# A two-pass convolution and expert kernel: the first two tiles of a pass as one stretch, the base copies moved, more half-channel stores

## The chip, the core and the metric

The kernel runs on one core of one Trainium2 chip. The metric is the device time of one execution in microseconds (us). Engines are named as the profile names them: PE (TensorE), PEld (its weight loads), DVE (VectorE), ACT (ScalarE), POOL (GpSimd), SP (SyncE, which here only issues DMAs).

## The reference, cut to what matters

Input `x` is 8 batches x 4096 positions x 512 channels in float32. Two steps follow one another.

```python
# step 1, on all of x: a long convolution per channel over the normalised input
x = x + conv(layernorm(x)) + layernorm(x) * omega      # 8 x 4096 x 512
# step 2, on 4096 tokens (1024 x 4) read from the result: two of eight experts per token
h  = gelu(xr @ w1A[e].T @ w1B[e]);  ye = h @ w2A[e].T @ w2B[e]
x  = x + y          # y: the weighted sum of the two experts, scattered to the tokens
```

(The experts' tokens are the first 4096 rows of the flattened array, which are all of batch 0. In the kernel `T` is 4096, and `o_tok` is the output seen as rows of 512 channels.)

## The kernel before, in words

**Passes, tiles, blocks, units.** The convolution is done in two passes `g` = 0 and 1, four batches each. A pass has four tiles `t` of 128 channels (DG = 4). A tile has 8 blocks `i` (BT = 8), a block has two units `k` of 8 channels, so 16 units a tile (UT = 16). `xb` has two halves; a tile lives in one half (128 partitions x 128 rows x 128 channels, 8 MB), is computed in place, and is stored from there, while the other half takes the next tile.

**One unit.** POOL and DVE each centre half of a unit's channels (L581, L1225, `cen`), DVE multiplies by the reciprocal deviation (L1236, `xn`), PE forms chunk sums (L1448) and local products (L1461), ACT shifts (L947) and builds tap matrices (L966, L967, L973), DVE scans the state (L1263), PE adds the part between chunks (L1473), and DVE adds the result into `xb` (L1247, the function `add`, which raises `s_ev` by one). In the loop the add of unit u-1 stands behind the scan of unit u. At the end of each tile DVE's function `steps` (with `end`) does the last add first and only then centres and stages the first unit of the next tile (L1272 on); PE's `over_halves` likewise closes the last unit of each tile before it starts the next. This is done for every tile of a pass, by `over_tile_blocks` and `over_halves`.

**SP's queue.** All tile loads and stores and the weights of the blocks are issued by SP in program order (`tile(g, t, first, final)`). A tile is moved in 16 pieces. In the first tile of a pass SP loads the next tile (16 pieces of 512 KB, L679) and then, once 8 units are added, stores the first 64 of the tile's 128 channels (16 half pieces of 256 KB, L786; runs of 64 channels are 256 bytes). In the second tile it waits for the 16th add of the first tile, stores the other halves (16 x 256 KB), and loads the third tile into the half that they leave. In the third tile it stores the second tile in whole pieces (16 x 512 KB, runs of 512 bytes, L696) and loads the fourth tile; each load waits for the store of its own piece (`s_put`). In the fourth tile it stores the third. Between the pieces stands a pair of weight loads per block (L736, 256 KB and L738, 128 KB).

**End of pass 0 and the experts.** In the fourth tile of pass 0 SP loads `w2a` (L769), stores four first halves into `y_d` (the rows the experts read, YP = 4 pieces) and issues three of the four base copies `copy_out` (L791: 1024 rows x 384 channels from `y_d` to `out`, 1.5 MB each); then `w1a` (L805), the slot table (L808) and, after the last add, the four second halves into `y_d` (L786). When they are there, POOL gathers the rows of the first two of 39 expert tiles (L613). An expert tile on PE is `turn`, `rank`, `up`, `down`, `widen`. DVE takes statistics of the gathered rows (`token_stats`, L1293), normalises them (L1302) and copies the rank result (`rank_in_half`, L1307, L1309), without which the next expert tile's `up` (L1556) cannot start. POOL's `tile(q)` scatters the result of tile q-3 to `out` (L548; at q = 3 only after all four base copies and four whole stores `store_last` have landed), then computes the deviation of tile q+2 (L621, L623) and gathers tile q+3 (L613), in this order. SP's `up_load(q)` waits until `up` of tile q-2 is done.

**End.** In the last tile of pass 1 SP stores the first 64 channels (16 half pieces) after 8 adds and the other 64 after the last add (the loop at L860).

## Time and profile before

| | us |
|---|---|
| median of 3 runs | 1139.38 |
| the three runs | 1147.12, 1139.38, 1137.70 |
| the profiled execution's own time | 1141.59 |
| span in its trace | 1139.8 |

The profiled execution has 1.8 us outside the span and is 2.2 us above the median. Busy shares over the span: PE 81%, DVE 72%, ACT 69%, POOL 53%; the mean granted TensorE clock is 0.941 of full speed. Pass 0 runs from about 121 to 388 us, the experts from there to about 850, pass 1 from there to the end. In the profile's 40 slices each slice is 28.5 us, a digit is a tenth of the slice.

### The profile page before, as it was taken

Reading aid. Unit: us, or ns where it says so; the run is one execution under the profiler, and the core shown is the slowest. Engines: PE = TensorE matmul, PEld = TensorE weight load, DVE = VectorE, ACT = ScalarE, POOL = GpSimd, SP = SyncE. Lnnn points to the kernel's source line nnn. Section 1 sums busy time; section 2 is a strip of 40 time slices with the busy share of each in tenths; the row PEclk is TensorE's granted clock in tenths of the full one; section 3 lists DMA queues with packets and bytes.
Section 4 is the critical chain, followed back from the end, with each engine's and each line's share of the span. In section 5 each row is a group of like instructions: output and inputs, shape, how many; then the busy total and the mean of one; then the engine's idle time right before and its main releaser. Section 6 shows DMA issues by size and latency. Waiting matters only on the chain. (4 is left out here: it accounts for less than half of the span.)

```text
span 1139.8 us, 32813 instructions
## 1 busy us (share of the span) xinstructions
PE 921.1 (81%) x11452; PEld 745.4 (65%) x11452; DVE 815.8 (72%) x1360; ACT 784.9 (69%) x1151; POOL 602.2 (53%) x674
## 2 busy tenths in 40 slices
PE   2770588879858858999999999999987888885882
PEld 1540477767747746777777777777766777774671
DVE  6877897988859533565767767776657989795891
ACT  2782698979949734656565566565667989896890
POOL 4334785868755133656666666665665433331330
PEclk9995798999979979999999999999999999898896
DMA  7999799999999986999999999899749999999986
GB/s 254 387 401 334 198 264 220 259 251 287 265 287 322 266 211 182 240 262 290 275 267 245 230 249 245 225 251 233 177 107 263 221 207 265 268 291 255 312 191 150
DMA packets 391625, 288.01 MB, mean 253 GB/s; under 512 B 125416, under 2 KB 339080, under 8 KB 391042
## 3 DMA queue, kind: packets, MB, share of 16 engines
q1 hardware_dynamic: 347458, 211.88, 69.9%
q0 software_dynamic: 19520, 36.26, 14.6%
q10 hardware_dynamic: 24576, 38.94, 10.5%
q8 instruction: 43, 0.70, 0.3%
q14 instruction: 28, 0.23, 0.1%
HBM read 197.41 MB, written 100.61 MB: 261 GB/s over the span
## 5 line engine op out<-in xcount | busy, mean ns | idle before, releaser
L1461 PE MATMUL ps<-xn,wb 128*128 128x128 f32 x2048 | 275.4, 290 | 0.0
L1062 ACT ACTIVATE cen<-ps 128x1024 f32<-128x1024 f32 x156 | 155.8, 1024 | 169.1 <-PE ps L1556 169.0
L581 POOL TENSOR_TENSOR cen<-xb,mean 128x512 f32<-128x512 f32 x128 | 143.0, 1118 | 228.5 <-DVE state L1263 160.9
L1461 PEld LDWEIGHTS ps<-xn,wb 128*128 128x128 f32 x2048 | 250.6, 200 | 17.4 <-issue 3.1
L1236 DVE TENSOR_TENSOR xn<-cen,rstd 128x1024 f32<-128x1024 f32 x128 | 174.5, 1363 | 51.0 <-POOL cen L581 39.4
L1448 PE MATMUL ps<-xn,near 128*32 128x128 f32 x2048 | 86.8, 289 | 134.4 <-DVE xn L1236 84.9
L1556 PE MATMUL ps<-carry,wb 64*128 64x256 f32 x1248 | 168.7, 400 | 13.0 <-DVE carry L1309 10.9
L1571 PE MATMUL ps<-cen,xn 128*64 128x128 f32 x2496 | 160.4, 276 | 0.4 <-ACT cen L1062 0.3
L1571 PEld LDWEIGHTS ps<-cen,xn 128*64 128x64 f32 x2496 | 135.9, 137 | 37.7 <-ACT cen L1062 30.7
L1247 DVE TENSOR_TENSOR xb<-xb,ps 128x1024 f32 (+1 forms) x128 | 152.9, 1194 | 9.9 <-PE ps L1473 9.9
L966 ACT ACTIVATE wb<-wide 32x1024 f32<-32x1024 f32 x126 | 144.4, 1146 | 16.6 <-DMA wide<-taps_d 14.0
L1448 PEld LDWEIGHTS ps<-xn,near 128*32 128x32 f32 x2048 | 52.4, 113 | 157.3 <-issue 73.8
L1556 PEld LDWEIGHTS ps<-carry,wb 64*128 64x128 f32 x1248 | 112.5, 188 | 42.5 <-issue 25.6
L1293 DVE BATCH_NORM_STATS2 tstat<-wide 128x6 f32<-128x512 f32 x78 | 53.9, 694 | 118.4 <-DMA wide<-y_d,pick_g 118.4
L967 ACT ACTIVATE wb<-wide 32x768 f32<-32x768 f32 x126 | 114.8, 911 | 1.5
L613 POOL DMA_INDIRECT wide<-y_d,pick_g x78 | 89.1, 1142 | 46.5 <-POOL pick_g L610 34.6
L465 POOL DMA_INDIRECT slot_d<-rowf,posi x64 | 103.2, 1613 | 10.4 <-issue 10.3
L1225 DVE TENSOR_TENSOR cen<-xb,mean 128x512 f32<-128x512 f32 x128 | 91.4, 714 | 17.1 <-DMA xb<-L_attn_x 17.1
L1473 PE MATMUL ps<-state,carry 32*128 32x128 f32 x2048 | 93.5, 297 | 0.0
L1094 DVE BATCH_NORM_STATS2 wb<-xb 128x512 f32 (+1 forms) x128 | 78.5, 679 | 18.8 <-DMA xb<-L_attn_x 18.4
L947 ACT ACTIVATE shift_s<-ps,coef 128x124 f32<-128x124 f32 x128 | 45.5, 356 | 64.5 <-PE ps L1448 63.4
L1473 PEld LDWEIGHTS ps<-state,carry 32*128 32x128 f32 x2048 | 69.0, 186 | 25.1 <-issue 24.1
(173 smaller groups left out, 1262.0 us busy)
## 6 DMA issues: line engine op xcount, KB each, us to landing
xb<-L_attn_x SPq DMA_DIRECT2D x96, 512.0 KB
out<-xb SPq DMA_DIRECT2D x72, 512.0 KB, 6.5
xb<-L_attn_x SPq DMA_DIRECT2D x32, 1024.0 KB, 10.0
xb<-L_attn_x ACTq DMA_DIRECT2D x128, 256.0 KB, 4.9
out<-xb SPq DMA_DIRECT2D x88, 256.0 KB, 4.5
wb<-L_ffn_w_B SPq DMA_DIRECT2D x78, 256.0 KB, 4.5
wide<-taps_d SPq DMA_DIRECT2D x62, 256.0 KB, 6.1
dk<-decay_d SPq DMA_DIRECT2D x62, 128.0 KB, 5.4
```

The lines of the kernel that those rows point to most:

```text
L465: pool.indirect_dma_start(out=slot_d, out_offset=bass.IndirectOffsetOnAxis(ap=pos_col[:, c:c + 1], axis=0), in_=row_col[:, 2 * c:2 * c + 2 ...
L581: pool.tensor_tensor(cen[:, k, 0:QB // 2].rearrange("p b r d -> p r b d"), unit_view(pool, g, i, k)[:, :, 0:UC // 2] .rearrange("p r (b d) ...
L966: act.activation(dst[0:ZR], src, ACT.Copy)
L967: act.activation(dst[ZR:2 * ZR, :, :, ZR:P], src[:, :, :, 0:P - ZR], ACT.Copy).then_inc(s_rev, 1)
L1062: act.activation(act_h[:, b % 2].rearrange("p f t -> p (f t)"), ps[:, 2 * (b % 2):2 * (b % 2) + 2, :].rearrange("p a t -> p (a t)"), ACT.G ...
L1236: dve.tensor_tensor(xn[:, k].rearrange("p (b d) r -> p b d r", d=2), cen[:, k].rearrange("p b r d -> p b d r"), rstd[:, g * P:(g + 1) * P] ...
L1247: dve.tensor_tensor(view, view, ps[:, QB * k:QB * k + QB, 0:2 * P] .rearrange("p b (d r) -> p r b d", d=2), ALU.add).then_inc(s_ev, 1)
L1448: ins = pe.matmul(ps[b * 2 * N:(b + 1) * 2 * N, QB * k, 2 * P:3 * P], near[:, h, k * QB + b, d:d + 2, :].rearrange("p z n -> p (z n)"), xn ...
L1461: ins = pe.matmul(ps[:, QB * k + b, d * P:(d + 1) * P], wb[:, h, k * QB + b, d, :], xn[:, k, 2 * b + d, :], start=(b > 0 and d == 0), stop ...
L1473: ins = pe.matmul(ps[:, QB * k + b, d * P:(d + 1) * P], carry[rows, k, d * P:(d + 1) * P], state[rows, k, :], start=False, stop=True, skip ...
L1556: ins = pe.matmul(ps[:, 2 * (b % 2) + h, f * QT:(f + 1) * QT].rearrange("p (a t) -> p a t", a=2), w1bs[half_rows, k, c * P:(c + 1) * P], r ...
L1571: ins = pe.matmul(ps[h * RANK:(h + 1) * RANK, 4, 0:P], w2as[:, (f // 2) * (FC // 2) + 2 * b + f % 2, :], act_h[:, b % 2, f, side * P:(side ...
```

## The change

Three things are changed.

1. `RUNS = ((0, 2), (2, 3), (3, 4))`: DVE and PE run through the first two tiles of each pass as one loop; the stretch's closing steps stand after tile 2, 3 and 4 of a pass, not after the first.
2. In the last block of the second tile SP issues the first halves of 8 of its 16 pieces (`SOON` = 8); in the third tile the other halves of these 8 pieces follow in place of whole pieces. In the last tile of pass 1 the early part of a piece is 80 channels (`LASTC`), issued after 10 adds, and the late part 48.
3. The three base copies leave the fourth tile of pass 0; all four now stand between the `up_load`s of the first expert tiles, and the four `store_last` stand in pairs behind the second and third of them.

```diff
+    SOON = PIECES // 2
+    LASTC = 5 * P // 8
...
+        RUNS = ((0, 2), (2, 3), (3, 4))
+
         def over_tile_blocks(eng, g, step):
 
-            for t in range(g * DG, (g + 1) * DG):
-                step(t * BT, True, False)
-                with eng.Fori(t * BT + 1, (t + 1) * BT - 1) as i:
+            for a, z in RUNS:
+                i0, i1 = g * NK + a * BT, g * NK + z * BT
+                step(i0, True, False)
+                with eng.Fori(i0 + 1, i1 - 1) as i:
                     step(i, False, False)
-                step((t + 1) * BT - 1, False, True)
+                step(i1 - 1, False, True)
+
+        def halves_out(g, tile):
+
+            return 16 * (g * (PIECES + SOON + YP) + PIECES + (0, SOON, SOON, SOON + (YP, PIECES)[g])[tile])
...
-            pool.wait_ge(s_early, 16 * (PIECES + YP))
+            pool.wait_ge(s_early, halves_out(0, DG - 1))
...
-                second = t == g * DG + 1
+                second, third = t == g * DG + 1, t == g * DG + 2
...
-                        elif second and 0 <= j < PIECES:
+                        elif (second and 0 <= j < PIECES) or (third and 0 <= j < SOON):
                             store_part(g, t - 1, j, slice(P // 2, P), s_put[j])
                         elif not first and 0 <= j < PIECES:
                             store_tile(g, t - 1, [j])
                         elif PIECES <= j < 2 * PIECES and not first and not final:
-                            if second and j == PIECES:
-                                sp.wait_ge(s_early, 16 * (PIECES if g == 0 else 2 * PIECES + YP))
+                            if j == PIECES:
+                                sp.wait_ge(s_early, halves_out(g, t - 1 - g * DG))
                             load_tile(g, t + 1, [j - PIECES], stored(g, t - 1))
-                    if final and g == 0 and b >= BT // 2:
-                        if b == BT // 2:
-                            for j in range(PIECES):
-                                sp.wait_ge(s_put[j], 16 * t)
-                            for j in range(KC):
-                                sp.dma_start(load2a[:, j, :], w2a[j * P:(j + 1) * P, :]).then_inc(s_wl, 16)
-                            store_early(g, t, range(YP))
-                        else:
-                            copy_out(b - BT // 2)
+                    if second and b == BT - 1:
+                        for j in range(SOON):
+                            store_part(g, t, j, slice(0, P // 2), s_early)
+                    if final and g == 0 and b == BT // 2:
+                        for j in range(PIECES):
+                            sp.wait_ge(s_put[j], 16 * t)
+                        for j in range(KC):
+                            sp.dma_start(load2a[:, j, :], w2a[j * P:(j + 1) * P, :]).then_inc(s_wl, 16)
+                        store_early(g, t, range(YP), P // 2)
                     if final and g == 1 and b == BT - 1:
-                        store_early(g, t, range(PIECES))
-
-            def store_early(g, t, pieces):
-
-                sp.wait_ge(s_ev, UT * t + UT // 2)
+                        store_early(g, t, range(PIECES), LASTC)
+
+            def store_early(g, t, pieces, cols):
+
+                sp.wait_ge(s_ev, UT * t + cols // UC)
                 for j in pieces:
-                    store_part(g, t, j, slice(0, P // 2), s_early)
+                    store_part(g, t, j, slice(0, cols), s_early)
...
             sp.wait_ge(s_w2b, 32)
-            for j in range(YP):
-                store_last(j)
             copy_out(0)
             for q in range(2, 5):
                 up_load(q, q % 2)
+                copy_out(q - 1)
+                for j in range((q - 2) * YP // 2, min((q - 1) * YP // 2, YP)):
+                    store_last(j)
...
-                store_part(1, NT - 1, j, slice(P // 2, P), s_put[j])
-            sp.wait_ge(s_early, 16 * (YP + 3 * PIECES))
+                store_part(1, NT - 1, j, slice(LASTC, P), s_put[j])
+            sp.wait_ge(s_early, halves_out(1, DG - 1))
```

(PE's `over_halves` takes the same `RUNS`.)

SP's order around the turn from the second to the third tile of pass 0. `xb<-L_attn_x` is a piece of a tile load, `y_d<-xb` and `out<-xb` are stores, `x64` at the end of a shape is a half piece and `x128` a whole one, `wide` and `dk` are a block's weights. Before:

```order
L736 DMA wide<-taps_d 32x8x256
L738 DMA dk<-decay_d 128x256
L736 DMA wide<-taps_d 32x8x256
L738 DMA dk<-decay_d 128x256
L696 DMA y_d<-xb 128x8x128 x4
L736 DMA wide<-taps_d 32x8x256
L738 DMA dk<-decay_d 128x256
L696 DMA out<-xb 128x8x128 x5
```

Now:

```order
L745 DMA wide<-taps_d 32x8x256
L747 DMA dk<-decay_d 128x256
L795 DMA y_d<-xb 128x8x64 x4
L795 DMA out<-xb 128x8x64 x4
L745 DMA wide<-taps_d 32x8x256
L747 DMA dk<-decay_d 128x256
L795 DMA y_d<-xb 128x8x64 x4
L745 DMA wide<-taps_d 32x8x256
L747 DMA dk<-decay_d 128x256
L795 DMA out<-xb 128x8x64 x4
L705 DMA out<-xb 128x8x128
```

Eight half pieces stand ahead of the last weights of the second tile, and eight more take the place of eight whole ones behind them.

DVE's order at a turn between tiles (L1247 is `add`, L1263 the scan, L1225 `centre`, L1236 `stage`). Before, this stands behind every tile of a pass but the last:

```order
L1263 SCALAR_TENSOR_TENSOR state<-carry,shift_s 128x128
L1247 TENSOR_TENSOR xb<-xb,ps 128x128x8 x2
L1225 TENSOR_TENSOR cen<-xb,mean 128x128x2x2
L1236 TENSOR_TENSOR xn<-cen,rstd 128x1024
L1225 TENSOR_TENSOR cen<-xb,mean 128x128x2x2
L1236 TENSOR_TENSOR xn<-cen,rstd 128x1024
```

Now, between the first and the second tile, the loop's body runs on:

```order
L1246 TENSOR_TENSOR xn<-cen,rstd 128x1024
L1235 ISA
L1235 TENSOR_TENSOR cen<-xb,mean 128x128x2x2
L32 REGISTER_ALU
L1273 SCALAR_TENSOR_TENSOR state<-carry,shift_s 128x128
L32 REGISTER_ALU
L1257 ISA x2
L1257 TENSOR_TENSOR xb<-xb,ps 128x128x8
```

The 16th add of the first tile, which stood right behind the 15th, now stands behind the scan of the second tile's first unit.

SP's order at the start of the experts, from the `w2b` load (L833) on; `wb<-L_ffn_w_B` is a half of an `up_load`. Before (after the second `up_load`, with its four stores and one copy in one piece):

```order
L818 DMA wb<-L_ffn_w_B 64x1024
L823 DMA out<-xb 128x8x128 x4
L791 DMA out<-y_d 1024x384
L373 TENSOR_LOAD t_e
L373 ISA x2
L818 ISA
L818 DMA wb<-L_ffn_w_B 64x1024
```

Now, from the same `up_load` to the third copy:

```order
L800 DMA out<-y_d 1024x384
L375 TENSOR_LOAD t_e
L375 ISA x2
L827 ISA
L827 DMA wb<-L_ffn_w_B 64x1024
L827 ISA
L827 DMA wb<-L_ffn_w_B 64x1024
L800 DMA out<-y_d 1024x384
L832 DMA out<-xb 128x8x128 x2
L375 TENSOR_LOAD t_e
```

The fourth copy now stands behind `up_load(4)`, so behind SP's wait for the `up` of the third expert tile.

## Rows read from the trace of the kernel before

**Rows 1.** The page, part 2: DMA, 40 slices of 28.5 us, tenths.

```profile
DMA  7999799999999986999999999899749999999986
```

**Rows 2.** Timeline, DVE, first turn of pass 0 (start, us, instruction, idle before).

```profile
178.61 0.86 DVE L1263 TENSOR_TENSOR_SCAN state<-carry,shift_s 128x128 f32<-128x128 f32 x1
...
184.81 1.22 DVE L1247 TENSOR_TENSOR xb<-xb,ps 128x1024 f32<-128x1024 f32 x1 [1.22 <-PE ps L1473]
...
198.77 0.42 DVE L1263 TENSOR_TENSOR_SCAN state<-carry,shift_s 128x128 f32<-128x128 f32 x1
...
202.63 0.41 DVE L1263 TENSOR_TENSOR_SCAN state<-carry,shift_s 128x128 f32<-128x128 f32 x1
```

**Rows 3.** Timeline, DVE, first turn of pass 1.

```profile
911.94 0.41 DVE L1263 TENSOR_TENSOR_SCAN state<-carry,shift_s 128x128 f32<-128x128 f32 x1
...
917.69 1.22 DVE L1247 TENSOR_TENSOR xb<-xb,ps 128x1024 f32<-128x1024 f32 x1 [1.10 <-PE ps L1473]
...
927.13 0.41 DVE L1263 TENSOR_TENSOR_SCAN state<-carry,shift_s 128x128 f32<-128x128 f32 x1
...
934.51 0.41 DVE L1263 TENSOR_TENSOR_SCAN state<-carry,shift_s 128x128 f32<-128x128 f32 x1
```

**Rows 4.** Timeline, POOL and DVE, the second turns of both passes.

```profile
247.84 1.10 POOL L581 TENSOR_TENSOR cen<-xb,mean 128x512 f32<-128x512 f32 x1 [4.66 <-DMA xb<-L_attn_x]
...
248.81 1.22 DVE L1247 TENSOR_TENSOR xb<-xb,ps 128x1024 f32<-128x1024 f32 x1 [1.28 <-PE ps L1473]
...
979.21 2.16 POOL L581 TENSOR_TENSOR cen<-xb,mean 128x512 f32<-128x512 f32 x2 [5.49 <-DMA xb<-L_attn_x]
...
980.48 1.22 DVE L1247 TENSOR_TENSOR xb<-xb,ps 128x1024 f32<-128x1024 f32 x1 [1.09 <-PE ps L1473]
```

**Rows 5.** Timeline, DVE, the third turns of both passes.

```profile
322.90 0.69 DVE L1225 TENSOR_TENSOR cen<-xb,mean 128x512 f32<-128x512 f32 x1 [8.15 <-DMA xb<-L_attn_x]
...
1053.93 0.69 DVE L1225 TENSOR_TENSOR cen<-xb,mean 128x512 f32<-128x512 f32 x1 [8.96 <-DMA xb<-L_attn_x]
```

**Rows 6.** Windows: stretch, engines' busy time, PEclk, DMA share, GB/s (last two).

```profile
187.00:248.00 61.00, 54.32 (x756) 46.20 (x756) 52.91 (x62) 56.25 (x79) 44.12 (x37) 0.94 1.11 257
248.00:251.00 3.00, 0.66 (x17) 0.47 (x16) 2.19 (x2) 1.17 (x2) 2.81 (x3) 1.00 0.20 47
251.00:323.00 72.00, 54.88 (x768) 46.68 (x768) 55.33 (x65) 57.14 (x80) 45.57 (x39) 0.91 1.11 275
979.00:983.00 4.00, 1.33 (x23) 1.02 (x21) 2.82 (x4) 2.01 (x3) 2.16 (x2) 0.90 0.71 155
1056.00:1082.00 26.00, 21.98 (x307) 18.64 (x308) 23.21 (x27) 22.49 (x32) 8.90 (x10) 0.91 1.09 315
1121.00:1138.00 17.00, 0.00 (x0) 0.00 (x0) 0.00 (x0) 0.00 (x0) 0.00 (x0) 0.53 0.97 216
```

**Rows 7.** Timeline, SP, the second halves into `y_d`, behind the three base copies.

```profile
387.80 7.86 SPq L786 DMA_DIRECT2D y_d<-xb  x4
```

**Rows 8.** Timeline, POOL, the first gather and the first scatter.

```profile
398.60 0.19 POOL L610 COPY pick_g<-slot_g 128x2 int32<-128x2 int32 x1 [19.33 <-DMA y_d<-xb]
...
454.77 0.20 POOL L541 COPY pick_s<-slot_s 128x2 int32<-128x2 int32 x1
```

**Rows 9.** Timeline, PE and DVE, the third expert tile and `rank_in_half(5)`.

```profile
442.17 3.08 PE L1556 MATMUL ps<-carry,wb 64*128 64x256 f32 x16 [4.46 <-DVE carry L1309]
...
450.78 1.13 PE L1556 MATMUL ps<-carry,wb 64*128 64x256 f32 x8
...
474.50 0.29 DVE L1307 COPY carry<-ps 128x128 f32<-128x128 f32 x1 [1.04 <-PE ps L1541]
```

**Rows 10.** Source L791 (the four base copies), issue to landing.

```profile
DMA to landing us min/median/max: 10.3/13.6/19.3
```

**Rows 11.** Timeline, DVE, the last tile: its 10th and 16th add.

```profile
1097.41 1.19 DVE L1247 TENSOR_TENSOR xb<-xb,ps 128x1024 f32 x1
...
1117.30 1.22 DVE L1247 TENSOR_TENSOR xb<-xb,ps 128x1024 f32<-128x1024 f32 x1 [1.42 <-PE ps L1473]
```

More of the change, by code:

```diff
@@ L76, in build @@
     YP = CH // PR
-    assert YP % 2 == 0
+    assert YP % 2 == 0 and DG == 4
+    SOON = PIECES // 2
+    LASTC = 5 * P // 8
     ZR = P // 4
@@ L567, in tile_start @@
             def tile_start(i, g):
-                return isinstance(i, int) and i % BT == 0 and i != g * NK
+                return i - g * NK in [a * BT for a, _ in RUNS[1:]]
             def centres(g):
@@ L1487, in over_halves @@
             def over_halves(g):
-                for t in range(g * DG, (g + 1) * DG):
-                    steps(t * BT, 0, True)
-                    with pe.Fori(t * BT // 2, (t + 1) * BT // 2 - 1) as p:
+                for a, z in RUNS:
+                    i0, i1 = g * NK + a * BT, g * NK + z * BT
+                    steps(i0, 0, True)
+                    with pe.Fori(i0 // 2, i1 // 2 - 1) as p:
                         steps(p * 2 + 1, 1)
                         steps(p * 2 + 2, 0)
-                    steps((t + 1) * BT - 1, 1)
-                    between((t + 1) * BT - 1, 1)
+                    steps(i1 - 1, 1)
+                    between(i1 - 1, 1)
             pe.wait_ge(s_late, NLATE)
```

## The prediction

> **What bounds the kernel now.** I read the slices first [rows 1]. DMA stands at 9 tenths or more in nearly every slice of both passes, which makes its queue the first suspect, but a share says nothing of who waits. Then the turns between tiles.
>
> *First turn* [rows 2, 3]. DVE scans once a unit: 198.77 and 202.63 are one unit apart, 3.86 us; 927.13 and 934.51 two units, 3.69 us each. From the scan at 178.61 to the one at 202.63 are five units: 24.0 us instead of 19.3, so the turn costs 4.7 us. In pass 1, 911.94 to 934.51 is 22.6 instead of 18.4: 4.1 us. This is what the run-through can take away, 8.8 us together.
>
> *Second turn* [rows 4]. POOL centres the first unit of the third tile as soon as its load has landed: it waited for the DMA until 247.84, and the last add of the second tile ended at 250.03. In pass 1: 979.21 and 981.70. The loads are there only 2.2 and 2.5 us before the compute wants them.
>
> *Third turn* [rows 5]. Here the compute waits in earnest: DVE has idled 8.15 us, its adds all done, when the fourth tile's load lands at 322.9, and 8.96 us in pass 1 at 1053.9. So each pass is set by the DMA at its third turn, and whatever is won before it is lost in this wait unless the loads land earlier too.
>
> *What sets these loads* [rows 6]. The window 187 to 248, in which SP stores halves and loads the third tile, has a DMA share of 1.11 throughout, and so has 251 to 323. Between them, 248 to 251, it is 0.20: SP waits for the last add. The queue is a chain of work: last add of tile 1, second halves, load of tile 3, a short hole, stores of tile 2, load of tile 4.
>
> **The change, part by part.**
>
> *1. The run-through, first effect: the last add is later.* In the loop the add of unit 15 stands behind the scan of unit 16. Pass 0: 178.61 is the scan of unit 14, two units later is 186.3, the add starts 0.3 behind it, 186.6 instead of 184.81 [rows 2]: 1.8 us later. Pass 1: 911.94 + 7.4 + 0.3 = 919.6 instead of 917.69 [rows 3]: 2.0 us later. SP waits for this add before its second halves, and behind them stand the loads of the third tile, on a full queue. So these land at 247.84 + 1.8 = 249.6, and at 981.2. The second tile's compute ends 4.7 us earlier (4.1), at about 245.3 and 977.6, and now waits for the loads: of the 8.8 us nothing is left but some 1 us at the start of the third tile, which the third turn's wait absorbs.
>
> *2. The hole closes.* The second tile's last add (245.3) is now earlier than the end of the loads, and SP has issued eight half stores as well. It is worth, by the windows, 3 x (1 - 0.20/1.11) = 2.5 us in pass 0 and 4 x (1 - 0.71/1.11) = 1.4 us in pass 1 [rows 6]. The run-through alone would have closed it.
>
> *3. Eight pieces in halves.* A half store costs 16 x 256 KB at 216 GB/s, 1.21 us each, with only such stores running (1121 to 1138) [rows 6]. For a whole one I compare the two chains of a pass, which differ only in 16 whole for 16 half stores: last add to landed load, 186.03 to 247.84 is 61.8 us and 250.03 to 322.9 is 72.9, in pass 1 60.3 (918.91 to 979.21) and 72.2 [rows 2 to 5] (an add lasts 1.22); so a whole one costs 0.69 to 0.74 us more than a half, about 1.93. Two halves are 2.42, 0.5 us more. Eight pieces: 4.0 us a pass. Ends: a whole piece at the 315 GB/s of the window 1056 to 1082 is 1.66 us, so 0.76 x 8 = 6.1 us; and 0, if in the mixed stream bytes alone count, as nearly in the first window (257 GB/s with 16 half stores in it, against 275). I take 4.0, from the stretch in which these stores will stand.
>
> What the rows give for two halves against a whole is 2.42 against 1.93 at the least. The Trainium skill (DMA: Bandwidth & Descriptors, Why small descriptors are slow) counts a fixed 3 cycles per descriptor beside one per 32 bytes, so 22 for two halves against 19; by it, an estimate, term 3 would be 2.4 us a pass (1.93 x 3/19 x 8) and the whole sum 3.2 us less. The trace asks for more, and the measurement decides.
>
> Third turn: pass 0 1.8 - 2.5 + 4.0 = **+3.3 us**, pass 1 2.0 - 1.4 + 4.0 = **+4.6 us**. Where the compute idled 8 to 9 us at this turn it will idle 15 to 17: the TensorE clock, 0.91 over these windows, will fall for longer, which costs nothing that isn't in the turn already.
>
> *4. Base copies out of the fourth tile.* They are ahead of the four `y_d` halves, whose issue took 7.86 us on the full queue [rows 7] and whose landing released the first gather at 398.60 [rows 8], 10.8 us after the last add. On an empty queue four halves need 0.9 + 4 x 1.21 + 1.0 = 6.7 us (start and tail as at the kernel's end: last add 1118.5, 16 x 1.21, end 1139.8 [rows 11]): 394.5. The slot table and PE's transposes, which the gather needs too, may then be the later ones; I allow 0.6 us: 395.1. Gain **-3.5 us**; ends -2 (the `w1a` load still ahead) and -4.5.
>
> *5. The copies in the expert loop.* SP issues, behind `w2b`, copy, `up_load(2)`, copy, two stores: 0.5 MB more ahead of the gather for tile 3 than four stores and one copy, on a queue which already holds PE up by 4.46 us before 442.17 [rows 9]. At 250 to 290 GB/s that is 1.8 us; between 0 and 3 I take **+1.0**. The rest of the copies go against a wait: POOL's first scatter (454.77 [rows 8], now 452.3 by the two terms) waits for all four. The fourth is behind `up_load(4)`, which waits for the `up` that ended at 451.9 [rows 9], now 449.4; issued at 451.5. The four copies took 10.3 to 19.3 us to land, 13.6 in the middle [rows 10]; the quickest had 1 MB of halves (4.8 us) ahead, the new one 0.5 MB of `up_load` (1.9 us), so 7.4 at least; I take 9: 460.5. POOL stands still 8 us, and behind it in its queue are the deviation of tile 5 and the gather of tile 6. DVE takes that gather's statistics before `rank_in_half(5)`, which PE needs for the next expert tile. The slack there is 1.04 us of DVE idle at 474.50 [rows 9]; I allow 2.2 us for a quicker landing on an emptier queue and for PE's own lag behind DVE's copies: 460.5 - 452.3 = 8.2, less 1.0 and 2.2, gives some **+4.5 us**, once, since POOL keeps pace afterwards. Ends 0 (it lands with the 452.3) and +9.
>
> *6. The last stores.* The early part may start after the 10th add, 1098.6 [rows 11], two units later than before, and then fills the queue until the last add: 1098.6 + 0.9 + 16 x (80-channel + 48-channel run) + 1.0. On a line through 1.21 us for 256 bytes and 1.66 to 1.93 for 512 the two are together 2.42: 38.7 us, end 1139.2 against 1139.8: **-0.6 us**. Ends: -1.5, if the early run is done when the last add ends, and +3 (rival D).
>
> Instruction counts otherwise fall by a few waits; the half stores' extra SP issues stand beside a full queue and cost nothing of their own.
>
> Sum: 3.3 + 4.6 - 3.5 + 1.0 + 4.5 - 0.6 = **+9.3 us**. Against the median of 1139.4 that is **1148.7 us**; the profiled execution before, 1141.6, lies 2.2 above its median and would become 1150.9.
>
> **The rivals.**
>
> *A. The halves cost nothing and the copies are hidden (0.2).* Terms 3 and 5 at their lower ends: -0.7 + 0.6 - 3.5 - 0.6 = -4.2, 1135.2; with the scatter wait alone 1140. For it: the mixed windows move nearly the same GB/s.
>
> *B. Faster: the compute, not the queue, sets the third turn (0.1).* If the loads move up with the compute, because SP's order is paced by the block's weights and not by a full queue, both turns come off: -8.8 - 3.5 - 0.6 = -12.9, 1126.5. It decides if the third tile's loads would land more than 4 us earlier than the compute asked for them; the rows say 2.2 and 2.5 and a share of 1.11.
>
> *C. Slower (0.12).* A half store is worth its 1.21 and a whole one 1.66, +12.2 for both passes, and the scatter waits 9 us: +18, 1157. It decides if the fourth copy lands later than about 462.
>
> *D. The last runs don't divide (0.08).* If a 48-channel run costs what a 64-channel run does (1.21 us a piece) and an 80-channel one 1.4, a fifth of the way from 1.21 to 1.93 and more, the end is 16 x 2.61 = 41.8 us after the start, 3.1 later than with 38.7: 1151.8. No row has such a run. The Trainium skill (DMA: Bandwidth & Descriptors, How a descriptor splits into AXI transactions) speaks for this case: a read starts at a 256-byte boundary and is billed for the bytes ahead of its own start, and the late run begins at byte 320 of a 512-byte row.
>
> *E.* That the run-through does nothing, because the second tile's loads aren't there, is out: SP issues them in the first four blocks of the first tile, half a tile ahead of the turn.
>
> **The numbers.** The forecast itself has 0.5, from 1143 to 1155. The range that should hold 8 in 10 is 1136 to 1158: from A's end to C. 1% of 1139.4 is 11.4 us, about what can be told from no change. Faster than 1128: B, 0.10. Slower than 1150.8: two fifths of the forecast's half (0.2), C and half of D, 0.36. Within 1%: the rest, 0.54.
>
> **What would show it.** The wait of DVE for the load at the third turns grows from 8 and 9 us to about 15, with the loads landing 3 to 5 us later after the pass's start; the DMA hole at the second turn is gone. The last add before the second halves comes 2 us later. The first gather starts 7.3 us after the last add of pass 0 instead of 10.8. POOL's first scatter waits some 8 us for the DMA, and PE stalls by 4 to 5 us before its sixth expert tile. Wrong would be: loads that land earlier at the third turn (then B), a scatter that doesn't wait, or an end more than 21 us behind the last add.

## The result, and the profile after

The changed kernel took **1156.77 us** (median of 4 runs, 1156.35 to 1157.85), the one before 1141.73 (4 runs, 1137.7 to 1147.12): a ratio of 1.013, with an interval of 1.0083 to 1.0178. So it is slower, by 15 us, where 1148.7 was forecast and the range ended at 1158. The profiled execution took 1157.0 with a span of 1155.2; the span before was 1139.8. The 15.4 us between the two spans are what is explained here.

The page first, part 2: busy tenths in 40 slices, the granted clock and the DMA.

```profile
span 1155.2 us, 33019 instructions
...
PEclk9995799989969979899999999999999999897896
DMA  7999899999999489889999999899749989999969
```

The DMA row is as full as it was [rows 1]. It can't show what changed; one line of part 3 can. Of the kernel's 408258 packets 158440 are below 512 bytes, and before there were 125416: 33024 more, and 32768 of them are the half pieces (16 whole pieces of 1024 runs each have become two halves of 1024 runs).

The second turn of pass 0: DVE's last add of the second tile, then the load it waits for (start, us, instruction, and in brackets the idle time before it with what ended it).

```profile
245.19 1.22 DVE L1257 TENSOR_TENSOR xb<-xb,ps 128x1024 f32<-128x1024 f32 x1 [1.30 <-PE ps L1483]
250.90 0.69 DVE L1235 TENSOR_TENSOR cen<-xb,mean 128x512 f32<-128x512 f32 x1 [4.49 <-DMA xb<-L_attn_x]
250.95 1.59 POOL L590 TENSOR_TENSOR cen<-xb,mean 128x512 f32<-128x512 f32 x1 [11.39 <-DMA xb<-L_attn_x]
```

The run-through did what it says. The tile's last add starts at 245.19 instead of 248.81 [rows 4] (245.3 was forecast), and DVE then stands still for 4.49 us, because the load lands at 250.9 instead of 247.8. The gain of the first turn is handed over to the queue within one tile.

The third turns, pass 0 and pass 1, from the last add on.

```profile
314.50 1.22 DVE L1257 TENSOR_TENSOR xb<-xb,ps 128x1024 f32<-128x1024 f32 x1 [0.93 <-PE ps L1483]
330.04 0.69 DVE L1235 TENSOR_TENSOR cen<-xb,mean 128x512 f32<-128x512 f32 x1 [14.31 <-DMA xb<-L_attn_x]
...
1054.04 1.22 DVE L1257 TENSOR_TENSOR xb<-xb,ps 128x1024 f32<-128x1024 f32 x1 [1.09 <-PE ps L1483]
1067.23 0.69 DVE L1235 TENSOR_TENSOR cen<-xb,mean 128x512 f32<-128x512 f32 x1 [11.97 <-DMA xb<-L_attn_x]
```

These answer to [rows 5]: 8.15 us of waiting have become 14.31, and 8.96 have become 11.97. Windows of the same stretches (busy time of PE, PEld, DVE, ACT and POOL, then granted clock, DMA share, GB/s):

```profile
190.00:251.00 61.00, 49.30 (x724) 41.97 (x720) 50.38 (x59) 54.14 (x76) 44.21 (x35) 0.97 1.14 257
251.00:330.00 79.00, 53.85 (x768) 45.83 (x768) 55.83 (x64) 57.56 (x80) 50.69 (x40) 0.89 1.07 252
```

Against [rows 6] the same 768 matmuls now stand in 79 us instead of 72, the DMA share is 1.07 for 1.11, and the queue moves 252 GB/s where it moved 275. Nothing of the hole of 3 us is left (248 to 251 us has a share of 1.17, where it had 0.20), and still the load lands later.

The start of the expert loop: SP's halves into `y_d` behind the last add, and POOL's first gather.

```profile
394.85 2.92 SPq L795 DMA_DIRECT2D y_d<-xb  x4
402.40 0.18 POOL L619 COPY pick_g<-slot_g 128x2 int32<-128x2 int32 x1 [16.09 <-DMA y_d<-xb]
```

The issue of the four second halves takes 2.92 us instead of 7.86 [rows 7], and the gather starts 7.6 us behind the last add (394.82) instead of 10.8 [rows 8]. Then the fourth base copy on SP, POOL's first scatter, which waits for it, and DVE and PE at the sixth expert tile.

```profile
456.51 0.59 SPq L800 DMA_DIRECT2D out<-y_d  x1
...
465.06 0.18 POOL L550 COPY pick_s<-slot_s 128x2 int32<-128x2 int32 x1 [3.32 <-DMA out<-y_d]
...
481.10 0.69 DVE L1303 BATCH_NORM_STATS2 tstat<-wide 128x6 f32<-128x512 f32 x1 [1.83 <-DMA wide<-y_d,pick_g]
...
485.10 1.23 PE L1567 MATMUL ps<-carry,wb 64*128 64x256 f32 x4 [5.41 <-DVE carry L1319]
```

The scatter had no wait before [rows 8]. PE's third expert tile (its `up`, at 443.86) is 41.5 us behind the first gather instead of 43.6, the fourth (458.11) 55.7 instead of 56.0, and the sixth 82.7 instead of 77.5: all of the loss stands at the sixth. The copies now took 8.4 to 14.0 us to land, 10.1 in the middle; before 10.3 to 19.3 [rows 10].

Last, the stores at the end: the last add, and two windows, one with the 80-channel parts and one with the 48-channel parts.

```profile
1131.08 1.22 DVE L1257 TENSOR_TENSOR xb<-xb,ps 128x1024 f32<-128x1024 f32 x1 [1.42 <-PE ps L1483]
```

```profile
1120.00:1132.00 12.00, 10.36 (x160) 8.81 (x159) 8.75 (x10) 6.27 (x11) 1.60 (x2) 1.00 1.29 240
...
1134.00:1154.00 20.00, 0.00 (x0) 0.00 (x0) 0.00 (x0) 0.00 (x0) 0.00 (x0) 0.51 0.96 166
```

A 48-channel part holds 192 KB, so at 166 GB/s it takes 1.18 us, hardly less than the 1.21 us of a 64-channel part with its 256 KB [rows 6]. An 80-channel part takes 320 KB / 240 GB/s = 1.37 us. (Here 1 KB is 1024 bytes and 1 GB is 10^9.) The end comes 22.9 us behind the last add, 21.3 before.

Where the 15.4 us are, read from the same marks in both traces:

| stretch | before | after | change | sum |
|---|---|---|---|---|
| up to the first add of pass 0 | 131.84 | 133.10 | +1.3 | 1.3 |
| to the landed load of the fourth tile | 322.95 | 330.09 | +5.9 | 7.1 |
| to the first gather | 398.60 | 402.40 | -3.3 | 3.8 |
| to the sixth expert tile on PE | 476.13 | 485.10 | +5.2 | 9.0 |
| to the first add of pass 1 | 859.39 | 869.96 | +1.6 | 10.6 |
| to the landed load of the fourth tile | 1053.97 | 1067.28 | +2.7 | 13.3 |
| to the last add's end | 1118.52 | 1132.30 | +0.5 | 13.8 |
| to the end of the span | 1139.8 | 1155.2 | +1.6 | 15.4 |

The first row lies ahead of anything that was changed, so a row of such a table is uncertain by 1 us at the least. In the expert loop it is more: a second profile of the same kernel (the last experiment) has the sixth expert tile 87.2 us behind the gather where this one has 82.7.

The lower granted clock (0.930 over the span, 0.941 before) isn't a cause. From its landed load to its last add the fourth tile of pass 0 took 64.8 us before and 64.7 after, and in pass 1 64.6 and 65.0.

### The profile page after: what moved, and what is told of

It reads as the page before. It is cut to its first block and busy times, and to the rows that moved or that the text cites. A ratio compares the mean times of both kernels' runs of the same rounds, so it can differ in the third digit from the quotient of the medians.

```text
span 1155.2 us, 33019 instructions
## 1 busy us (share of the span) xinstructions
PE 921.4 (80%) x11452; PEld 744.5 (64%) x11452; DVE 817.4 (71%) x1360; ACT 784.8 (68%) x1151; POOL 609.2 (53%) x674
## 2 busy tenths in 40 slices
DMA packets 408258, 287.91 MB, mean 249 GB/s; under 512 B 158440, under 2 KB 355720, under 8 KB 407682
## 3 DMA queue, kind: packets, MB, share of 16 engines
q1 hardware_dynamic: 364098, 211.88, 70.8%
q10 hardware_dynamic: 24576, 38.94, 10.3%
## 5 line engine op out<-in xcount | busy, mean ns | idle before, releaser
L1246 DVE TENSOR_TENSOR xn<-cen,rstd 128x1024 f32<-128x1024 f32 x128 | 177.1, 1384 | 45.6 <-POOL cen L590 38.6
L474 POOL DMA_INDIRECT slot_d<-rowf,posi x64 | 109.6, 1713 | 10.6 <-issue 10.6
```

Of the source, the lines that this page charges most:

```text
L474: pool.indirect_dma_start(out=slot_d, out_offset=bass.IndirectOffsetOnAxis(ap=pos_col[:, c:c + 1], axis=0), in_=row_col[:, 2 * c:2 * c + 2 ...
L1246: dve.tensor_tensor(xn[:, k].rearrange("p (b d) r -> p b d r", d=2), cen[:, k].rearrange("p b r d -> p b d r"), rstd[:, g * P:(g + 1) * P] ...
```

## The experiments

Three sets of four kernels. The kernel before, run beside each set, took 1139.27, 1154.44 and 1162.03 us, so times are compared only as ratios to it; 0.01 is 11.4 us in the first set and 11.6 in the third. Most of the difference between the sets lies in the expert loop: from the sixth expert tile to the first add of pass 1 the kernel before needs 383.3 us, the one divided by rows, in the third set, 400.1. Why, no run shows; that the first and the third set bear the same chip number speaks against the chip. A diff is against the changed kernel unless it says otherwise. "Copies as before" is

```diff
-                    if final and g == 0 and b == BT // 2:
+                    if final and g == 0 and b >= BT // 2:
...
+                        else:
+                            copy_out(b - BT // 2)
...
+            for j in range(YP):
+                store_last(j)
             copy_out(0)
             for q in range(2, 5):
                 up_load(q, q % 2)
-                copy_out(q - 1)
-                for j in range((q - 2) * YP // 2, min((q - 1) * YP // 2, YP)):
-                    store_last(j)
```

### Set 1: the parts, one by one

**The run-through alone** (copies as before, and)

```diff
-    SOON = PIECES // 2
-    LASTC = 5 * P // 8
+    SOON = 0
+    LASTC = P // 2
```

> The kernel before with the run-through of the first two tiles of each pass alone: whole pieces, last stores 64/64 and base copies as before. Queue theory (the DMA queue sets the third turn): the 8.8 us of compute come off but are lost in the wait for the fourth tile's loads; third turn -0.7 us in pass 0 and +0.6 in pass 1, so the time is that of before within 2 us, and DVE's idle before the fourth tile grows from 8 and 9 us to 12 or 13. Rival (the compute sets it): 8 to 9 us faster than before.

Measured 1138.08 us, 0.998 (0.9957 to 1.0002). POOL at the second and the third turn of pass 0:

```profile
249.61 1.59 POOL L590 TENSOR_TENSOR cen<-xb,mean 128x512 f32<-128x512 f32 x1 [11.51 <-DMA xb<-L_attn_x]
...
320.37 1.59 POOL L590 TENSOR_TENSOR cen<-xb,mean 128x512 f32<-128x512 f32 x1 [12.63 <-DMA xb<-L_attn_x]
```

The first load lands 1.8 us later than in [rows 4], just what the later add costs, and the second one 2.6 us earlier than in [rows 5]. Of the 8.8 us of the two first turns nothing reaches the time that can be told from none. The idle time was expected wrongly, though. DVE waits 4.61 us at the second turn, where it had no wait, and 5.72 and 6.72 us at the third turns, not 12 or 13: it is done with the third tile at 314.6 us where the kernel before was at 314.7, because what the first turn gave was already handed back at the second.

**No early halves** (everything else as changed)

```diff
-    SOON = PIECES // 2
+    SOON = 0
```

> The changed kernel with its extra half stores undone (no first halves in the second tile's last block, whole pieces in the third tile). If two halves cost 0.5 us more than a whole piece: 8 us faster than the changed kernel, about 1.1490 ms where that is at 1.1568; from the third turns measured after the change (5.8 and 3.1 us late instead of the 3.3 and 4.6 forecast) 8 to 10 us. If the halves cost nothing and it is their order or the later last add that holds the loads: the time of the changed kernel within 2 us.

Measured 1143.15 us, 1.0031 (1.001 to 1.0052). Against 1.013 of the changed kernel some 0.01 is gone, 11 us, with nothing but the eight half pieces of each pass. The fourth tile's load in pass 0:

```profile
323.62 1.59 POOL L590 TENSOR_TENSOR cen<-xb,mean 128x512 f32<-128x512 f32 x1 [13.58 <-DMA xb<-L_attn_x]
...
458.75 0.18 POOL L550 COPY pick_s<-slot_s 128x2 int32<-128x2 int32 x1 [5.71 <-DMA out<-y_d]
```

The load lands 6.5 us earlier than the changed kernel's. The wait of the scatter stays, so it belongs to the copies.

**The last tile at 64 and 64**

```diff
-    LASTC = 5 * P // 8
+    LASTC = P // 2
```

> The changed kernel with its last stores of pass 1 split 64/64 channels again, the early part after 8 adds. In the trace after, an 80-channel part takes 1.37 us a piece (240 GB/s) and a 48-channel one 1.18 (166 GB/s), together 2.55 against 2.42, and the end came 22.9 us behind the last add instead of 21.3: 1.6 us faster than the changed kernel. If the split is worth what the forecast said, 0.6 us slower.

Measured 1154.87 us, 1.0156 (1.0134 to 1.0177), not to be told from the changed kernel's 1.013. The trace does tell: the last add ends at 1130.45 and the span at 1151.8, 21.4 us later, where the changed kernel has 22.9. The 80/48 division costs 1.5 us in its own place.

**The copies back**

> The changed kernel with the base copies where they were before (three in the fourth tile of pass 0, one behind the four whole stores). By the traces the move gained 3.3 us up to the first gather (7.6 us behind the last add instead of 10.9) and lost 5.2 up to the sixth expert tile, so undoing it gives 2 us, and no wait of the first scatter for a DMA. Rival: the 1.6 us that the later expert tiles lost too belong to it, then 3.5 us; or the loss has other grounds, then it gets 3 us slower.

Measured 1151.66 us, 1.0117 (1.0099 to 1.0135). The gather starts 10.1 us behind the last add, as before the change. POOL's first scatter:

```profile
456.33 0.19 POOL L550 COPY pick_s<-slot_s 128x2 int32<-128x2 int32 x1
```

No wait. The sixth expert tile is 77.9 us behind the first gather instead of 82.7. So by these traces the move wins 2.5 to 3.3 us at the gather and loses 4.8 to 5.2 behind it. The two times (1.0117 and 1.013) can't be told apart.

### Set 2: what a half piece costs, and the last runs

**Only the division.** The kernel before, but eight whole pieces of the third tile's stores are issued in place as two channel halves:

```diff
+                            if third:
+                                store_part(g, t - 1, j, slice(0, P // 2), s_early)
                             store_part(g, t - 1, j, slice(P // 2, P), s_put[j])
```

> The kernel before (no run-through, copies and last stores as before); in each pass's third tile 8 of the 16 pieces are stored as two halves, one right behind the other, at the place of the whole piece. It asks what the shorter runs cost by themselves. By the size alone, 0.5 us a piece as forecast: 8 us slower than before, the third turns 4.0 us later each. From the pair of kernels with and without early halves (third tile's load to fourth tile's load 79.1 against 71.7 us and 76.6 against 72.2): 7.4 and 4.5 us, 12 us slower. If the cost came from their place, right behind the loads, and not from their size: as before within 2 us.

Measured 1168.73 us, 1.013 (1.0091 to 1.0169): 15 us. The window of the stores, first of the kernel before and then of this one:

```profile
250.00:281.00 31.00, 25.76 (x352) 21.93 (x352) 27.04 (x32) 25.13 (x36) 22.40 (x21) 0.89 1.00 272
```

```profile
249.00:285.00 36.00, 31.55 (x416) 26.70 (x416) 32.58 (x38) 31.06 (x43) 31.02 (x24) 0.91 1.01 244
```

The same 16 pieces take 36 us instead of 31, with the engines as busy (1.01, 1.00) and fewer GB/s. That is 5 us, 0.63 a piece, in pass 0. By the landed loads it is 4.0 us in pass 0 (326.95 for 322.95) and 5.6 in pass 1 (80.4 us from the third tile's load to the fourth's, for 74.8). The time says 7.5 a pass; what the rest is isn't shown.

At the start of these stores the pieces into `y_d` are at the head of SP's queue, whole in the kernel before (first window) and halves here:

```profile
251.00:256.00 5.00, 2.83 (x24) 2.42 (x25) 4.79 (x6) 1.56 (x3) 1.51 (x2) 0.58 1.01 281
```

```profile
251.00:256.00 5.00, 5.00 (x44) 4.34 (x40) 3.50 (x5) 3.65 (x5) 3.28 (x4) 0.50 0.94 207
```

At 281 GB/s a whole piece takes 1.87 us, at 207 GB/s a half takes 1.27, so two halves are 0.67 us dearer.

**The early halves without the run-through** (copies as before, 64 and 64, and)

```diff
-        RUNS = ((0, 2), (2, 3), (3, 4))
+        RUNS = ((0, 1), (1, 2), (2, 3), (3, 4))
```

> The kernel before with the early halves alone (first halves of 8 pieces in the second tile's last block, second halves in the third tile; no run-through, copies and last stores as before). Size theory: the time of the kernel with the split alone, less the part of the hole at the second turn that the early halves fill (2.5 and 1.4 us by the windows, 4.3 and 3.0 by the run-through's own trace): between 3 and 8 us slower than before. Place theory: slower than the split alone. Were the halves free, as their place in the diff suggests, it would be 4 to 7 us faster than before.

Measured 1162.54 us, 1.0059 (1.0035 to 1.0083): 7 us. Where the first halves can fill the hole they cost less than in place, but they cost. (The two intervals don't overlap. In the traces the difference is in pass 1, 77.6 us from load to load for 80.4; in pass 0 the loads land at 326.55 and 326.95.) DVE and POOL stand still for 12.53 and 19.65 us at the third turn of pass 0, whose load lands at 326.55.

**The last tile in three parts** (the kernel before, with 64, 32 and 32 channels)

```diff
-    LASTC = 5 * P // 8
+    LASTC = 3 * P // 4
...
-                        store_early(g, t, range(PIECES), LASTC)
+                        store_early(g, t, range(PIECES), P // 2)
+                        sp.wait_ge(s_ev, UT * t + LASTC // UC)
+                        for j in range(PIECES):
+                            store_part(g, t, j, slice(P // 2, LASTC), s_early)
```

> The kernel before with the last tile of pass 1 stored in three parts: 64 channels after 8 adds, 32 after 12, the last 32 after the last add (runs of 256, 128 and 128 bytes; the middle one begins at byte 256 of a 512-byte row, the last at byte 384). It prices short runs. If a run costs by what it moves: each 32-channel part 0.6 to 0.8 us a piece, 10 to 13 us for 16, and the end 6 us earlier behind the last add than 21.3. If a short run costs what 256 bytes cost: 1.2 us both, 19 us each, and the end no earlier; as the middle part (issued at 1112, done at 1131) is then still running at the last add (1118.5), 10 us later. If reads start at 256-byte boundaries and nothing else counts: the middle part 0.8 us a piece, the last one 1.2.

Measured 1156.08 us, 1.0007 (0.9981 to 1.0033). Two windows, the first within the second parts (channels 64 to 95, which start at byte 256 of a row), the others within the last (96 to 127, byte 384):

```profile
1137.00:1139.00 2.00, 0.00 (x0) 0.00 (x0) 0.00 (x0) 0.00 (x0) 0.00 (x0) 0.84 1.12 169
...
1145.00:1147.00 2.00, 0.00 (x0) 0.00 (x0) 0.00 (x0) 0.00 (x0) 0.00 (x0) 0.50 1.13 171
```

Both move 170 GB/s, 0.77 us a part of 128 KB. A run of 128 bytes costs the same at either place. The Trainium skill (DMA: Bandwidth & Descriptors, How a descriptor splits into AXI transactions) would bill the part at byte 384 also for the 128 bytes ahead of it; this case doesn't show that. The last 16 parts need 12.3 us, but the 16 before them start only at about 1130, when the 64-channel parts are through, and so both stand behind one another in the last 25 us; the end is 19.7 us behind the last add (1135.8).

**One copy in the fourth tile, the last one behind the second `up_load`** (run-through, whole pieces, 64 and 64)

```diff
+                    if final and g == 0 and b == BT // 2 + 1:
+                        copy_out(1)
...
-            for q in range(2, 5):
+            for q in range(2, 4):
                 up_load(q, q % 2)
-                copy_out(q - 1)
-                for j in range((q - 2) * YP // 2, min((q - 1) * YP // 2, YP)):
+                copy_out(q)
+                for j in range((q - 2) * YP // 2, (q - 1) * YP // 2):
                     store_last(j)
+            up_load(4, 0)
```

> A version that may beat both: the run-through, whole pieces, last stores 64/64, one base copy left in the fourth tile of pass 0 and three in the expert loop, the last of them behind up_load(3) instead of up_load(4). Expected: the run-through alone (2 us faster than before), and 3 us more from the first gather (8 us behind the last add of pass 0 instead of 11), with no wait of the first scatter for a copy: 5 us faster than before. If the queue at the expert loop's start is the bound wherever the copies stand: as the run-through alone.

Measured 1153.0 us, 0.9966 (0.9939 to 0.9992). The gather and the scatter:

```profile
396.23 0.18 POOL L619 COPY pick_g<-slot_g 128x2 int32<-128x2 int32 x1 [16.25 <-DMA y_d<-xb]
...
455.16 0.19 POOL L550 COPY pick_s<-slot_s 128x2 int32<-128x2 int32 x1
```

The gather is 7.7 us behind the last add (388.49) and the scatter doesn't wait: both sides at once. No copy stands behind `up_load(4)` any longer, which waits for PE; but one copy fewer stands there, too, and no run has the one without the other. By the time this kernel can't be told from the run-through alone (0.998).

### Set 3: the copies alone, and what of a half piece costs

**The copies moved, nothing else** (as the run without early halves, and `RUNS` and `LASTC` as before)

> The kernel before with the base copies moved alone (all four and the paired whole stores between the up_loads; no run-through, whole pieces, last stores 64/64). Forecast's steps: 3.5 us won up to the first gather, 5.5 lost up to the sixth expert tile by the wait of the first scatter: 2 us slower than before. From the earlier pair with and without the move (the two kernels with run-through and whole pieces, less 1.6 us of last stores): 3.5 us slower. If the wait is harmless: 3 us faster.

Measured 1166.22 us, 1.0038 (1.0007 to 1.0069), 0.8 to 8 us.

```profile
394.37 0.19 POOL L619 COPY pick_g<-slot_g 128x2 int32<-128x2 int32 x1 [15.77 <-DMA y_d<-xb]
...
459.80 0.18 POOL L550 COPY pick_s<-slot_s 128x2 int32<-128x2 int32 x1 [8.06 <-DMA out<-y_d]
```

The scatter waits 8.06 us. So this part of the change is enough for the wait, and with the copies back there was none.

**The same eight pieces divided by rows**, not by channels: as many DMAs as in the run with the channel halves, but runs of 512 bytes.

```diff
-                            store_part(g, t - 1, j, slice(0, P // 2), s_early)
-                            store_part(g, t - 1, j, slice(P // 2, P), s_put[j])
+                            store_rows(g, t - 1, j, 0, s_early)
+                            store_rows(g, t - 1, j, 1, s_put[j])
```

> As the split-alone kernel, but each of the 8 pieces of a third tile is cut into two DMAs by rows (4 rows each, all 128 channels, runs of 512 bytes) instead of by channels. It tells the length of the runs from the number of DMAs: both kernels issue the same number of DMAs with the same bytes. If run length is what costs: as before within 2 us, where the split by channels was 1.3% slower. If each DMA on the full queue has a cost of its own: about as slow as the split by channels, 12 to 15 us.

Measured 1160.76 us, 0.9995 (0.9972 to 1.0019), and in the window of the stores:

```profile
249.00:285.00 36.00, 29.54 (x410) 25.32 (x411) 32.09 (x39) 30.27 (x43) 28.55 (x23) 0.95 0.99 272
```

272 GB/s, as undivided (the kernel before has 271 in the same window). Eight more DMAs a pass cost nothing that can be told; 256-byte runs in place of 512-byte ones are what costs 15 us.

**The best version** (the one-copy kernel, and of eight pieces 32 channels more after the 12th add)

```diff
                         store_early(g, t, range(PIECES), LASTC)
+                        sp.wait_ge(s_ev, UT * t + 3 * P // 4 // UC)
+                        for j in range(PIECES // 2):
+                            store_part(g, t, j, slice(LASTC, 3 * P // 4), s_early)
...
-                store_part(1, NT - 1, j, slice(LASTC, P), s_put[j])
+                store_part(1, NT - 1, j, slice(3 * P // 4 if j < PIECES // 2 else LASTC, P), s_put[j])
```

> The best of what the runs point to: run-through, whole pieces, one base copy left in the fourth tile of pass 0 (0.3% faster than before in the last call), and the last tile stored as 64 channels of all pieces after 8 adds, 32 channels of 8 pieces after 12 adds, the rest after the last add. A 32-channel part took 0.76 us a piece, so the 8 middle parts (6.1 us) fit between the end of the early ones and the last add, and behind it stand 8 x 0.76 + 8 x 1.21 = 15.8 us instead of 19.4: the end 17.7 us behind the last add instead of 21.3, 3.6 us more, 7 to 8 us faster than before in all. If the middle parts are still on the queue at the last add, the gain is less than 2 us.

Measured 1153.43 us, 0.9937 (0.9911 to 0.9963), 7 us faster than the kernel before. Against the one-copy kernel (0.9966) the times don't tell a gain, the trace does. The window behind the last add (which ends at 1133.51; the span ends at 1150.5):

```profile
1134.00:1149.00 15.00, 0.00 (x0) 0.00 (x0) 0.00 (x0) 0.00 (x0) 0.00 (x0) 0.52 1.13 201
```

The end is 17.0 us behind the last add, 21.3 before: 8 x 0.77 + 8 x 1.21 = 15.8 us of stores instead of 19.4.

**The changed kernel again**

> The changed kernel once more, on the chip on which the base copies alone are timed, since the chips differ by over a per cent in the time of the kernel before: 1.3% slower than before (interval of the first measurement 0.8 to 1.8%), 13 to 17 us; of these the copies alone 2 to 4.

Measured 1181.79 us, 1.0164 (1.0128 to 1.0199), with the third turn's load at 328.64 and a scatter that waits 6.87 us. The sixth expert tile is 87.2 us behind the gather.

## Why the prediction came out as it did

The time was in the range, near its upper edge, and the main mechanism was the forecast one: the queue sets the third turns, the halves cost it more than the hole gives, and the scatter waits for the moved copies. The greatest chance, 0.54, stood on a difference within 1%; what came, 1.3%, lay in the 0.36. The spans differ by 15.4 us where the sum was 9.3. By the table the 6.1 us between them are: the third turn of pass 0 +2.6 (5.9 for 3.3), the end +2.2 (1.6 for -0.6), the start and the rest of the expert loop, for which there was no term, +1.3 and +1.6, pass 1 up to its last add -1.4 (3.2 for 4.6), and the copies -0.2 (1.8 for 2.0).

**The run-through and the hole (1.8 - 2.5 and 2.0 - 1.4): right, nearly nothing is left.** Of the eight kernels whose runs stay at 512 bytes, the fourth tile's load of pass 0 lands at 320.4 to 323.8 in all, and the means are 322.8 with the run-through (four kernels) and 322.9 without it (the kernel before and three more). The forecast was -0.7. The load of the third tile came 1.8 us later, as forecast, once the 1.3 us at the start are taken off. From one load to the next the queue needs less without the hole than its share in a window told: with the run-through alone 70.8 and 71.8 us instead of 75.1 and 74.8, so 4.3 and 3.0 us, not 2.5 and 1.4. Not all of that is the hole: from 249 to 285 us, where the whole pieces are stored, the queue moves 284 to 298 GB/s in the five kernels without a hole and 271 to 280 in the three with one. Why isn't shown. One kernel without the run-through (the three parts), whose third load landed late, at 251.71, has 71.7 us as well; its hole was gone by itself. That fits a queue that sets both loads, and a hole that only takes up slack.

**The idle time at the third turns: one step counted twice.** The forecast had DVE wait 15 to 17 us there, the old 8 to 9 with the 4 to 5 us of the first turn and the later load on top. But its own step before had given the first turn's gain back at the second turn. So it came: DVE waits 4.49 and 4.66 us at the second turns, is done with the third tile at 315.7 us instead of 314.7, and the wait at the third turn grows only by what the load is late. It is 14.31 us in pass 0 because the load came 7.1 us later there, and 11.97 in pass 1. That the first is near the forecast's 15 is luck. The sum of the forecast didn't use this step.

**The halves (4.0 a pass): too little.** With early halves and the run-through (four profiles, two of them of the changed kernel) the fourth tile's load of pass 0 lands at 330.1, 328.5, 326.4 and 328.6, in the mean 328.4 and 5.6 us later than with whole pieces; measured from the third tile's load it is 78.1 us for 71.3, so 6.7. In pass 1 the way from the third tile's load to the fourth's is 76.6, 75.8, 75.2 and 76.0 with halves and 71.8, 72.2, 70.5 and 69.8 without: 4.8 us. That is 10.4 to 11.5 us for 8.0, or 0.6 to 0.8 us a piece; halves in place, without the run-through, cost 4.0 and 5.6. The forecast had 0.5 between bounds of 0 and 0.76. The times say 11 us by 1.013 against 1.0031, and 15 both by the halves in place and by the second measurement of the changed kernel (1.0164). So the term was right in kind and too small, and the measured price isn't firmer than these figures.

The price of a whole piece isn't one number, and that is the step that was too simple. By the two windows from 251 to 256 us, both behind a hole, a whole piece costs 1.87 us and not 1.93, and a half 1.27 and not 1.21: 0.67 a piece, 5.3 us a pass. Without the hole the whole pieces move faster, 284 to 298 GB/s from 249 to 285 us, but the kernels with early halves and the run-through have 234 to 241 there, no more than the 244 of the halves in place. So the halves also take away what the closed hole would have given, which fits their 6.7 us from load to load against 4.0 in place. The 1.93 came from two chains, 72.9 less 61.8 us [rows 2 to 5]. Both start on a queue that is idle for a microsecond, so that time falls out of the difference:

```profile
186.00:187.00 1.00, 0.00 (x0) 0.00 (x0) 0.91 (x3) 0.00 (x0) 0.00 (x0) 0.96 0.19 34
250.00:251.00 1.00, 0.00 (x0) 0.00 (x0) 1.00 (x2) 0.00 (x0) 0.97 (x2) 1.00 0.05 7
```

The rule of the Trainium skill that was weighed here (DMA: Bandwidth & Descriptors, Why small descriptors are slow), by which it would be 2.4 us a pass, an estimate, is further off than the rows were. It counts runs, not DMAs, and in that the run divided by rows agrees (0.9995).

**The copies (-3.5, +1.0, +4.5, together +2.0): the sum was right in the first trace, partly by luck.** The gather came 7.6 us behind the last add (7.3 forecast), and so it did in every kernel with the copies moved (7.3 to 7.6). The +1.0 for a later third expert tile didn't come: that tile was 2.1 us earlier behind the gather, and the fourth 0.3. All the loss stood at the sixth tile, where PE stood still for 5.41 us: 5.2 us later behind the gather, where the two terms had 5.5. And the scatter waited 3.32 us, where 8 was forecast. It started no later than forecast (62.7 us behind the gather; the forecast's 460.5 less 395.1 is 65.4), but POOL itself came to it 3.2 us later than before (59.3 us behind the gather for 56.2), since the statistics that its work ahead of the scatter needs came 3.0 us later; 3.2 and 3.32 together are the delay of the scatter. In the other kernels with the copies moved the scatter waits 3.8 to 8.1 us, and the sixth tile is 79.9 to 87.2 us behind the gather, where the kernels with the copies in their old place have 77.0 to 79.6.

The move costs more behind the sixth tile, for which no step was in the sum. In the first set the way from the first gather to the first add of pass 1 is 467.6, 465.1 and 464.4 us with the copies moved and 460.8, 459.2 and 459.0 without. That is 6.0 us in the mean, less 3.2 won at the gather, so 2.8. In the third set it is 483.9 (the copies alone) and 495.6 (the changed kernel again) against 477.0 (divided by rows), so the cost varies much from one profile to the next. By the time the copies alone cost 4.4 us, with an interval of 0.8 to 8, and the pair of run-through alone (0.998) and no early halves (1.0031) gives 5.8 less the 1.5 of the last stores, so 4.3.

**The last stores (-0.6): wrong, in sign.** An end more than 21 us behind the last add was a sign of being wrong, and it is 22.9. Rival D happened, by two thirds: the end came 1.6 us later by the table and 1.5 by the experiment, where D had +2.5. A line through 256 and 512 bytes was no way to price 192 and 320: they cost 1.18 and 1.37 us, together 2.55, where the line gave 2.42, and 16 of each make 2.1 us. The rule of the Trainium skill that was named beside D (DMA: Bandwidth & Descriptors, How a descriptor splits into AXI transactions), a run that is billed from the boundary ahead of it, agrees with the 192-byte run but not with the 32-channel parts, so it isn't shown.

**Rivals.** A (halves free, copies hidden) fell with the run without halves and with the scatter's wait. B (compute sets the third turn) fell with the run-through alone: the fourth tile's loads didn't follow the 4 to 5 us of the first turn (2.6 us earlier in pass 0 in that kernel, none in the mean of four), and the time shows no gain that can be told. C was the nearest in its total, 1157. Its price for a half piece, 0.76, and the forecast's 0.5 lie on either side of most of the measured ones (0.5 to 0.8 by the loads), and its scatter wait of 9 us is met by no run. The total was reached by D's stores and by 2.9 us that no case had, so it is luck that the time met C's.

## What to carry to other kernels

When a queue sets the time of a turn, a gain of the engines ahead of it is given back at the next load, and an edit that costs the queue more than the hole that it fills is a loss; so price the queue's items first, in the mix and at the fill of the queue in which they will stand. Divide a transfer along the dimension that keeps its runs long, and where it must be along the short one, measure each length: here 32 channels were worth dividing off and 48 were not. A transfer that another engine waits for should not stand behind an instruction on the same queue that itself waits for a late engine.

## What the runs showed of the hardware

- Stores from SBUF to DRAM with nothing else on the queues, by the length of a run: 128 bytes 170 GB/s, 192 bytes 166, 256 bytes 216. The 80-channel parts (320 bytes), which ran beside the last units' compute, moved at 240 GB/s. A 192-byte piece takes 1.18 us and a 256-byte piece 1.21, so a quarter fewer bytes gain next to nothing; a 128-byte piece takes 0.77.
- The DMA share says nothing of this: it is 1.00 at 272 GB/s with whole pieces and 1.01 at 244 GB/s with halves.
- In the same 5 us of two kernels, behind a stretch with an idle queue, stores in runs of 512 bytes moved at 281 GB/s and in runs of 256 bytes at 207. Where no such stretch lay ahead, the 36 us with the whole pieces moved at 284 to 298 GB/s, where one did, at 271 to 280.
- With a stretch of 3 us in which the queue was nearly idle, the way from one tile's load to the next took 75.1 us in the mean of three kernels, without it 71.3 in the mean of four. The second load landed at the same time in both (322.9 and 322.8), since without the hole the first one came later.
- Two DMAs for one, with the same bytes and runs of 512 bytes, for eight pieces a pass: 0.9995 (0.9972 to 1.0019), no change that can be told.
